# State-space stage: step sizes one state sooner; second mixer: the gates' logarithm first, query expansions behind the gate rows

## The chip, the cores and the metric

The kernel runs on one core of one Trainium2 chip. Times are device microseconds of one execution. The engines are TensorE (PE, matmuls; PEld is its weight load), VectorE (DVE), ScalarE (ACT), GpSimd (POOL) and SyncE (SP). Each works through its own list of instructions in order, and semaphores tie the lists together.

## The reference

A decoder of four layers, each with two mixers and a feed-forward part, over x of 16 x 128 tokens x 128 channels. Two of its parts are touched. The second mixer of layer 0 (the stage `l0_mlstm` of the kernel) is an attention whose weights come from gates:

```
log_fg = log_sigmoid(f_pre);  lf_cs = cumsum(log_fg)
log_d  = lf[..., 1:, None] - lf[..., None, 1:] + i_pre[..., None, :]   # causal
m      = max(log_d);  d_mat = exp(log_d - m)
s_mat  = (q k^T / sqrt(DH)) * d_mat
denom  = max(|sum(s_mat)|, exp(-m)) + eps;   out = s_mat v / denom
```

`f_pre` and `i_pre` are the forget and the input gate, each a matmul that is then capped with a tanh. The first mixer of layer 2 (the stage `l2_mamba`) is a selective state-space layer, 256 inner channels (two halves of 128) by 16 states:

```
xc = silu(conv(x_branch));  x_dbl = xc @ W_x      # dt_low, B, C
dt = sigmoid(dt_low @ W_dt + b_dt) * 0.099 + 0.001
h  = exp(dt * A) * h + (dt * xc) * B_t;   y_t = sum(h * C_t)
y  = (y + xc * D) * silu(z);   out = y @ W_out
```

## The kernel before, in words

The stages run one after the other. Between two stages all engines meet, so a stage starts when the last engine has ended the one before it. In each stage every engine has its list written out by hand, in the order of the code.

**The gates of `l0_mlstm`.** The block that ends the stage before holds `prepare` on VectorE, constants for this stage: zeros, biases, then `minus`, `a3`, `m3` and `thrice`, which are only needed once the rows are spread. Then the stage's own block starts. TensorE makes the forget gate (`gate = 1`), then the input gate (`gate = 0`) (L1878, 64 short matmuls a gate), then one score (L1888). ScalarE takes tanh of both (L2053), then Exp and Ln of the forget gate (L2057, L2059). VectorE makes the context's statistics (`c_stats`, two halves, L192 to L204), then the gate rows: the running sum `cs` (L2144), `a_row` (L2145), the running maximum `neg_m` (L2146), `floor_row` (L2147) and the sign of `neg_m` (L2148), which sets `rows_set`. GpSimd expands the queries, `q_pair`, in four instructions (L2316), with the two halves of `c_scales` (L212) ahead of the second and the third of them. TensorE fills its waits with matmuls whose result nobody reads, `keep_clock(n)` (L1903), then spreads `a_row` and `neg_m` (L1913), subtracts what ScalarE has rounded (L1920) in two parts, and turns `floor_row` (L1924); the exponents of batch 0 stand behind that in its list, and then the loop over 16 batches.

**The state-space stage.** The 16 batches go in four quarters `q` of 512 tokens, and in each quarter over 16 states `n`; `t = 16 q + n` counts the 64 steps. In a step VectorE runs one scan per half (L2707) and feeds the first half of the next step (`feed`, L2689; in every fourth step the second half as well, L2695); GpSimd feeds the second half (L2779) in the other steps and multiplies both halves by C (`read_out`, L2786); TensorE spreads B (`spread_b`, L2459) and C (`spread_c`, L2465) over the partitions and adds what GpSimd read out (`add_state`, L2480); ScalarE copies B and C from PSUM (L2612, L2617) and makes the decays (L2604). `feed(t)` on VectorE waits for ScalarE's copy of B, and on ScalarE that copy stands behind the copy of C of the step before.

Beside this, the steps of quarter `q` prepare quarter `q+1`: four taps of convolution a half (L2409, n = 4, 5, 8, 9), the tangent (L2565), `branch_x` on VectorE (L2672, L2562 on ScalarE), `x_bc` for B and C (L2427), `x_step` for the low-rank step size (L2433), its copy `take_xd` (L2592), `steps` (L2449), `tanh` (L2597), and `step_size` on VectorE (L2667), which makes `dtx`. GpSimd's feed of the first step of a quarter waits for the second half of `dtx`. The placement of each is a condition on `n`, as in TensorE's list:

```
if n == 11:
    x_bc(q + 1)
if n == 12:
    x_step(q + 1)
    take_high(q + 1, 0)
if n == 13:
    take_high(q + 1, 1)
    steps(q + 1, 0)
```

## Time and profile before

| | |
|---|---|
| median of 3 runs | 1565.3 us (1560.38 to 1567.12) |
| the profiled execution, its own time | 1562.59 us |
| its span in the trace | 1559.7 us, 28295 instructions |
| busy: PE, DVE, ACT, POOL | 1354.9, 1179.8, 879.3, 773.8 us (87, 76, 56, 50%) |
| mean granted TensorE clock | 0.944 of full speed |
| `l0_mlstm`, from its first gate matmul to the turn of `floor_row` | 157.01 to 179.41 us |
| state-space stage, from its first scan to its last | 726.5 to 968.6 us |

The profiled execution's own time is 2.9 us above its span (what lies around the first and the last instruction), and 2.7 us below the median of the three runs. A busy PE is not PE at its peak. No engine is busy throughout, so what a change is worth has to be read from the places where engines wait for each other.

### The profile page before, as it was taken

Reading aid. Unit: us, or ns where it says so; the run is one execution under the profiler, and the core shown is the slowest. Engines: PE = TensorE matmul, PEld = TensorE weight load, DVE = VectorE, ACT = ScalarE, POOL = GpSimd, SP = SyncE. Lnnn points to the kernel's source line nnn. Section 1 sums busy time; section 2 is a strip of 40 time slices with the busy share of each in tenths; the row PEclk is TensorE's granted clock in tenths of the full one; section 3 lists DMA queues with packets and bytes.
Section 4 is the critical chain, followed back from the end, with each engine's and each line's share of the span. In section 5 each row is a group of like instructions: output and inputs, shape, how many; then the busy total and the mean of one; then the engine's idle time right before and its main releaser. Section 6 shows DMA issues by size and latency. Waiting matters only on the chain. (4 is left out here: it accounts for less than half of the span.)

```text
span 1559.7 us, 28295 instructions
## 1 busy us (share of the span) xinstructions
PE 1354.9 (87%) x9646; PEld 885.0 (57%) x9646; DVE 1179.8 (76%) x2532; ACT 879.3 (56%) x2677; POOL 773.8 (50%) x740
## 2 busy tenths in 40 slices
PE   6997887899789998898988988899998678877895
PEld 3554555555567775563333432788887434436784
DVE  7997567789777785465898998777776787887654
ACT  4774342377677773225777775577766244343663
POOL 5667353222655442414988889433336222454553
PEclk9998898999999999999999999999999798878997
DMA  7000000000000000002000000000000400001353
GB/s 312 1 2 1 1 1 1 1 2 2 1 1 2 2 2 0 1 1 97 1 1 1 0 1 1 1 2 1 2 2 6 137 1 1 1 1 53 107 162 99
DMA packets 38494, 39.48 MB, mean 25 GB/s; under 512 B 2128, under 2 KB 35536, under 8 KB 37584
## 3 DMA queue, kind: packets, MB, share of 16 engines
q1 hardware_dynamic: 36304, 33.48, 6.5%
q0 software_dynamic: 2048, 4.20, 0.9%
q8 instruction: 78, 1.28, 0.3%
q14 instruction: 64, 0.52, 0.1%
HBM read 23.52 MB, written 14.16 MB: 24 GB/s over the span
## 5 line engine op out<-in xcount | busy, mean ns | idle before, releaser
L837 POOL TENSOR_TENSOR l_xattn_probs<-l_xattn_probs,l_xattn_recip 128x512 f32<-128x512 f32 x128 | 133.1, 1040 | 220.1 <-DVE l_xattn_recip L776 219.8
L1055 ACT ACTIVATE l_attn_probs<-ps,l_attn_neg_max 128x128 f32<-128x128 f32 x512 | 145.2, 383 | 64.0 <-DVE l_attn_neg_max L1126 62.7
L2786 POOL TENSOR_TENSOR l_mamba_hc<-l_mamba_h,l_mamba_c 128x512 f32<-128x512 f32 x128 | 159.0, 1270 | 0.0
L2707 DVE TENSOR_TENSOR_SCAN l_mamba_h<-ps,l_mamba_dBx 128x512 f32<-128x512 f32 x128 | 152.7, 1213 | 1.8 <-ACT ps L2604 0.7
L2480 PE MATMUL ps<-l_mamba_hc,w_const 128*128 128x512 f32 x256 | 136.3, 638 | 19.2 <-POOL l_mamba_hc L2786 16.5
L771 DVE COPY l_xattn_probsT<-ps 128x512 f32<-128x512 f32 x128 | 88.0, 687 | 69.7 <-PE ps L623 69.7
L246 POOL TENSOR_TENSOR rs<-rs,neg_half 128x4 f32<-128x4 f32 (+1 forms) x32 | 43.4, 1357 | 151.8 <-DVE rs L240 151.7
L722 ACT ACTIVATE l_xattn_probs<-ps,l_xattn_neg_max 128x128 f32<-128x128 f32 x256 | 91.8, 388 | 41.3 <-DVE l_xattn_neg_max L766 41.3
L722 ACT ACTIVATE l_xattn_probs<-l_xattn_biased,l_xattn_neg_max 128x128 f32<-128x128 f32 x256 | 99.3, 391 | 12.2 <-DVE l_xattn_neg_max L766 12.2
L2604 ACT ACTIVATE ps<-l_mamba_th,l_mamba_w_a_bias,l_mamba_w_a_scale 128x508 f32<-128x508 f32 x128 | 97.1, 782 | 13.4 <-DVE l_mamba_h L2707 12.9
L2480 PEld LDWEIGHTS ps<-l_mamba_hc,w_const 128*128 128x128 f32 x256 | 44.8, 194 | 86.7 <-POOL l_mamba_hc L2786 69.3
L623 PE MATMUL ps<-w_const,l_xattn_probs 128*128 128x128 f32 x512 | 81.7, 283 | 9.4 <-DVE l_xattn_probsT L771 5.3
L1126 DVE TENSOR_REDUCE l_attn_neg_max<-ps 128x8 f32<-128x1024 f32 x64 | 77.9, 1218 | 14.1 <-PE ps L926 13.9
L623 PEld LDWEIGHTS ps<-w_const,l_xattn_probs 128*128 128x128 f32 x512 | 57.4, 142 | 51.2 <-issue 39.3
L2779 POOL TENSOR_TENSOR l_mamba_dBx<-l_mamba_dtx,l_mamba_b 128x512 f32<-128x512 f32 x48 | 61.0, 1271 | 45.3 <-DVE l_mamba_dtx L2667 24.8
L1182 POOL TENSOR_TENSOR l_attn_probs<-l_attn_probs,l_attn_row_recip 128x1024 f32<-128x1024 f32 x32 | 60.7, 1896 | 40.6 <-DVE l_attn_row_recip L1074 40.6
L937 PEld LDWEIGHTS ps<-w_const,l_attn_probs 128*128 128x128 f32 x512 | 56.4, 142 | 42.2 <-issue 30.1
L937 PE MATMUL ps<-w_const,l_attn_probs 128*128 128x128 f32 x512 | 69.3, 279 | 7.9 <-DVE l_attn_probsT L1141 6.0
L615 PE MATMUL ps<-l_xattn_k,l_xattn_q 64*128 64x128 f32 x1024 | 74.4, 285 | 1.6 <-ACT xnT L381 0.9
L926 PE MATMUL ps<-l_attn_k_one,l_attn_q 32*128 32x512 f32 x256 | 73.1, 647 | 0.0
L615 PEld LDWEIGHTS ps<-l_xattn_k,l_xattn_q 64*128 64x128 f32 x1024 | 62.1, 187 | 11.8 <-issue 8.0
L261 POOL TENSOR_SCALAR xn<-x,mean,rs 128x128 f32<-128x128 f32 x67 | 56.2, 849 | 10.8 <-POOLq L123 8.7
(595 smaller groups left out, 3638.3 us busy)
## 6 DMA issues: line engine op xcount, KB each, us to landing
sorted_in<-l_nothing SPq DMA_DIRECT2D x4, 1344.0 KB, 11.5
sorted_out<-l_wide SPq DMA_DIRECT2D x8, 512.0 KB, 3.9
w_early<-in_l_moe SPq DMA_DIRECT2D x1, 3688.0 KB, 12.0
l_large<-sorted_in SPq DMA_DIRECT2D x4, 576.0 KB, 6.3
w_l_xattn<-in_l_xattn SPq DMA_DIRECT2D x1, 2176.0 KB, 18.7
l_large<-sorted_in SPq DMA_DIRECT2D x4, 512.0 KB, 4.4
w_early<-in_l_xattn SPq DMA_DIRECT2D x1, 1890.0 KB, 11.8
sorted_out<-l_wide SPq DMA_DIRECT2D x4, 320.0 KB, 2.6
```

The source lines that it names most:

```text
L615: mm = nc.tensor.matmul(S_of(D, n)[:, i * P:(i + 1) * P], q_sb[rows, b % 2, c, :], k_sb[rows, b % 2, c if own else 0, :], start=True, stop ...
L623: mm = nc.tensor.transpose(T_of(n)[:, g * P:(g + 1) * P], probs[:, D % 2, n, g, :], G.c["ident"])
L722: ins = nc.scalar.activation(probs[:, D % 2, n, g, :], values, ACT.Exp, bias=neg_max[:, D % 2, n, g:g + 1], accum_out=row_sum[:, D % 2, n, ...
L771: nc.vector.tensor_copy(probsT[:, D % 2, n, :, :], heads4(T_of(n))).then_inc(copied, 1)
L837: nc.gpsimd.tensor_tensor(probs[:, D % 2, n, :, :], probs[:, D % 2, n, :, :], along(recip[:, D % 2, n, :], [P, HALF, P]), ALU.mult).then_i ...
L937: mm = nc.tensor.transpose(T_all[:, g * P:(g + 1) * P], probs[:, t % 4, g, :], G.c["ident"])
L1055: ins = nc.scalar.activation(probs[:, t % 4, g, :], S_of(t)[:, g * P:(g + 1) * P], ACT.Exp, bias=neg_max[:, t % 2, g:g + 1], accum_out=total)
L1126: nc.vector.tensor_reduce(neg_max[:, t % 2, :], by_head(S_of(t), 8), AX.X, ALU.max, negate=True).then_inc(maxed, 1)
L2480: nc.tensor.matmul(G.ps[:, SUM_BANK[half], :], G.c["ident"], hc[:, t % 4, half, :], start=False, stop=n == NS - 1).then_inc((sum0, sum1)[h ...
L2604: nc.scalar.activation(bank4(DA_BANK[half])[:, :, 1:], th[:, q % 2, half, :, 1:], ACT.Exp, scale=a_scale[:, half, n:n + 1], bias=a_bias[:, ...
L2707: nc.vector.tensor_tensor_scan(flat(h[:, t % 2, half, :, :]), G.ps[:, DA_BANK[half], :], flat(dBx[:, t % 2, half, :, :]), 0.0, ALU.mult, A ...
L2786: nc.gpsimd.tensor_tensor(heads4(hc[:, t % 4, half, :]), h[:, t % 2, half, :, :], c_sb[:, t % 3, :, :], ALU.mult).then_inc((hc0_set, hc1_s ...
```

## The change

It has two parts. In `l0_mlstm`, the second half of `prepare` moves into VectorE's own list of the stage (`prepare_split`), ScalarE takes the forget gate through tanh, Exp and Ln before the tanh of the input gate, VectorE sets `rows_set` before it makes `floor_row` and makes the second half of the context's statistics after the rows, GpSimd's second, third and fourth `q_pair` wait until the rows are made, and TensorE has 6 instead of 14 `keep_clock` matmuls and starts to spread `a_row` before `neg_m` is there.

```diff
+        def prepare_split(dve):
+            link = Link(dve, prepared, 2)
             for n in range(2):
                 link.note(nc.vector.tensor_scalar(minus[:, n, :], G.c["ident"][0:R3, 0:R3], -1.0, None, ALU.mult))
             link.catch()
...
             score(0)
-            pe.wait_ge(gates_set, 2)
-            keep_clock(14)
-            pe.wait_ge(rows_set, 1)
+            pe.wait_ge(gates_set, 1)
+            keep_clock(6)
             for n, row in enumerate((a_row, neg_m)):
+                if n == 0:
+                    pe.wait_ge(own, 2)
+                else:
+                    pe.wait_ge(rows_set, 1)
...
-            for n, gate in enumerate((gate_f, gate_i)):
-                act.wait_ge(gates_made, n + 1)
-                nc.scalar.activation(gate[:], G.ps[:, G_BANK[1 - n], 0:P], ACT.Tanh, bias=bias15[:, 1 - n:2 - n],
-                                     scale=1.0 / CAP).then_inc(gates_set, 1)
+            act.wait_ge(gates_made, 1)
+            nc.scalar.activation(gate_f[:], G.ps[:, G_BANK[1], 0:P], ACT.Tanh, bias=bias15[:, 1:2], scale=1.0 / CAP).then_inc(gates_set, 1)
             act.wait_ge(gates_set, 1)
-
             nc.scalar.activation(gate_f[:], gate_f[:], ACT.Exp, scale=-CAP).then_inc(gates_set, 1)
-            act.wait_ge(gates_set, 3)
+            act.wait_ge(gates_set, 2)
             nc.scalar.activation(gate_f[:], gate_f[:], ACT.Ln, bias=1.0).then_inc(logs_set, 1)
+            act.wait_ge(gates_made, 2)
+            nc.scalar.activation(gate_i[:], G.ps[:, G_BANK[0], 0:P], ACT.Tanh, bias=bias15[:, 0:1], scale=1.0 / CAP).then_inc(gates_set, 1)
...
-            for half in range(2):
-                c_stats(dve, half)
+            prepare_split(dve)
+            c_stats(dve, 0)
             dve.wait_ge(logs_set, 1)
-            dve.wait_ge(gates_set, 2)
             link(nc.vector.tensor_tensor_scan(cs[:], G.ones[:, 0:P], gate_f[:], 0.0, ALU.mult, ALU.add))
+            dve.wait_ge(gates_set, 3)
             link(nc.vector.scalar_tensor_tensor(a_row[:], gate_i[:], CAP, cs[:], ALU.mult, ALU.add))
             link(nc.vector.tensor_tensor_scan(neg_m[:], zeros[:], a_row[:], NEG, ALU.add, ALU.max))
-            link(nc.vector.tensor_tensor(floor_row[:], cs[:], neg_m[:], ALU.subtract))
-            nc.vector.tensor_scalar(neg_m[:], neg_m[:], -1.0, None, ALU.mult).then_inc(rows_set, 2)
+            nc.vector.tensor_scalar(neg_m[:], neg_m[:], -1.0, None, ALU.mult).then_inc(rows_set, 1)
+            dve.wait_ge(rows_set, 1)
+            nc.vector.tensor_tensor(floor_row[:], cs[:], neg_m[:], ALU.add).then_inc(rows_set, 1)
+            c_stats(dve, 1)
...
-                if q in (1, 2):
-                    c_scales(pool, q - 1)
+                if q == 1:
+                    c_scales(pool, 0)
+                    pool.wait_ge(rows_set, 2)
+                if q == 3:
+                    c_scales(pool, 1)
```

In the state-space stage, `x_bc` is split in its two halves and starts one state sooner, `x_step`, `take_xd`, `steps`, `tanh` and `step_size` come one state sooner, the second tangent follows its copy in state 9 and VectorE's use of it comes between the two scans of state 10; and `spread_c` goes ahead of the second of a step's two `add_state`.

```diff
-                if n == 0 and q > 0:
-                    add_state(t - 2, 1)
-                    add_state(t - 1, 0)
                 if n == 3:
                     add_state(t - 2, 0)
-                if n >= 3:
+                if n >= 3 or (n == 0 and q > 0):
                     add_state(t - 2, 1)
-                    add_state(t - 1, 0)
                 if t < LAST:
                     spread_c(t + 1)
+                if n >= 3 or (n == 0 and q > 0):
+                    add_state(t - 1, 0)
...
+                    if n == 10:
+                        x_bc(q + 1, 1)
                     if n == 11:
-                        x_bc(q + 1)
+                        x_bc(q + 1, 0)
+                        x_step(q + 1)
                     if n == 12:
-                        x_step(q + 1)
                         take_high(q + 1, 0)
+                        steps(q + 1, 0)
                     if n == 13:
                         take_high(q + 1, 1)
-                        steps(q + 1, 0)
-                    if n == 14:
                         steps(q + 1, 1)
...
-                    if n in (7, 10):
-                        tangent_x({7: 1, 10: 0}[n])
-                    if n == 12:
+                    if n in (7, 9):
+                        tangent_x({7: 1, 9: 0}[n])
+                    if n == 11:
                         take_xd(q + 1)
-                    if n in (13, 14):
-                        tanh(q + 1, n - 13)
+                    if n in (12, 13):
+                        tanh(q + 1, n - 12)
...
-                if n == NS - 1 and q + 1 < NQ:
-                    step_size(q + 1, 1)
                 if t < LAST:
                     feed(t + 1)
+                if n == 10 and q + 1 < NQ:
+                    branch_x(q + 1, 0)
                 scan(t, 1)
-                if n == NS - 2 and q + 1 < NQ:
-                    step_size(q + 1, 0)
+                if n in (NS - 3, NS - 2) and q + 1 < NQ:
+                    step_size(q + 1, n - (NS - 3))
```

How the built instructions stand, at three places. First, ScalarE from the end of the stage before to the turn of the rows, before:

```order
L487 COPY xnT<-ps 128x512 x4
L123 UNCONDITIONAL_BRANCH
L2049 UNCONDITIONAL_BRANCH
L2053 ACTIVATE l_mlstm_gate_f<-ps,l_mlstm_bias 128x128
L2053 ACTIVATE l_mlstm_gate_i<-ps,l_mlstm_bias 128x128
L2057 ACTIVATE l_mlstm_gate_f<-l_mlstm_gate_f 128x128
L2059 ACT_TABLE_LOAD
L2059 ACTIVATE l_mlstm_gate_f<-l_mlstm_gate_f 128x128
L2066 CAST l_mlstm_high<-ps 96x512 x4
L2069 CAST l_mlstm_a<-ps 96x512
L2069 CAST l_mlstm_m<-ps 96x512
L2071 ACT_TABLE_LOAD
```

The same place in the changed kernel:

```order
L2058 ACTIVATE l_mlstm_gate_f<-ps,l_mlstm_bias 128x128
L2060 ACTIVATE l_mlstm_gate_f<-l_mlstm_gate_f 128x128
L2062 ACT_TABLE_LOAD
L2062 ACTIVATE l_mlstm_gate_f<-l_mlstm_gate_f 128x128
L2064 ACT_TABLE_LOAD
L2064 ACTIVATE l_mlstm_gate_i<-ps,l_mlstm_bias 128x128
L2071 CAST l_mlstm_high<-ps 96x512 x4
L2074 CAST l_mlstm_a<-ps 96x512
L2074 CAST l_mlstm_m<-ps 96x512
L2076 ACTIVATE l_mlstm_floor_row<-l_mlstm_floor_row 128x128
```

There are two loads of a function table in both. The first stays ahead of the Ln; the second has moved from the Exp of `floor_row` to the tanh of the input gate.

Second, GpSimd in the same stretch, before:

```order
L2316 TENSOR_TENSOR l_mlstm_q_pair<-xnT,w_const 128x1024
L209 MEMSET l_mlstm_neg_half 128x16
L212 TENSOR_TENSOR l_mlstm_rs<-l_mlstm_ve,l_mlstm_neg_half 128x8
L2316 TENSOR_TENSOR l_mlstm_q_pair<-xnT,w_const 128x1024
L212 TENSOR_TENSOR l_mlstm_rs<-l_mlstm_ve,l_mlstm_neg_half 128x8
L2316 TENSOR_TENSOR l_mlstm_q_pair<-xnT,w_const 128x1024 x2
```

The same place in the changed kernel:

```order
L2326 TENSOR_TENSOR l_mlstm_q_pair<-xnT,w_const 128x1024
L209 MEMSET l_mlstm_neg_half 128x16
L212 TENSOR_TENSOR l_mlstm_rs<-l_mlstm_ve,l_mlstm_neg_half 128x8
L2326 TENSOR_TENSOR l_mlstm_q_pair<-xnT,w_const 128x1024 x2
L212 TENSOR_TENSOR l_mlstm_rs<-l_mlstm_ve,l_mlstm_neg_half 128x8
L2326 TENSOR_TENSOR l_mlstm_q_pair<-xnT,w_const 128x1024
```

The second and third expansion now stand together behind a wait for the rows, and the second half of the scales has moved one expansion down.

Third, TensorE in states 11 to 13 of a quarter (L2480 adds a state, L2465 spreads C, L2459 spreads B, L2427 is `x_bc`, L2433 `x_step`, L2440 `take_high`, L2449 `steps`), before:

```order
L2465 MATMUL ps<-l_mamba_bc,rows_bf 128x512
L2427 MATMUL ps<-l_mamba_xc,l_mamba_w_w_bc 96x512 x2
L2459 MATMUL ps<-l_mamba_bc,rows_bf 128x512
L2480 MATMUL ps<-l_mamba_hc,w_const 128x512 x2
L2465 MATMUL ps<-l_mamba_bc,rows_bf 128x512
L2433 MATMUL ps<-l_mamba_xc,w_l_mamba 128x512 x2
L2440 MATMUL ps<-l_mamba_high,l_mamba_w_minus 96x512
L2459 MATMUL ps<-l_mamba_bc,rows_bf 128x512
```

States 10 to 12 in the changed kernel, where these lines are L2490, L2475, L2469, L2436 and L2443:

```order
L2490 MATMUL ps<-l_mamba_hc,w_const 128x512
L2436 MATMUL ps<-l_mamba_xc,l_mamba_w_w_bc 96x512
L2469 MATMUL ps<-l_mamba_bc,rows_bf 128x512
L2490 MATMUL ps<-l_mamba_hc,w_const 128x512
L2475 MATMUL ps<-l_mamba_bc,rows_bf 128x512
L2490 MATMUL ps<-l_mamba_hc,w_const 128x512
L2436 MATMUL ps<-l_mamba_xc,l_mamba_w_w_bc 96x512
L2443 MATMUL ps<-l_mamba_xc,w_l_mamba 128x512 x2
L2469 MATMUL ps<-l_mamba_bc,rows_bf 128x512
```

The spread of C now stands between the two additions of a step, and three matmuls of preparation (half of `x_bc`, both of `x_step`) stand ahead of state 12's spread of B, where there were two.

## Rows read from the trace of the kernel before

**Rows 1.** Timeline of VectorE, gate rows: start us, us, engine, line, what [idle before <-releaser]

```profile
155.31 0.31 DVE L1852 TENSOR_SCALAR l_mlstm_minus<-w_const 96x96 bf16<-96x96 f32 x2
...
165.22 0.42 DVE L2144 TENSOR_TENSOR_SCAN l_mlstm_cs<-ones,l_mlstm_gate_f 128x128 f32<-128x128 f32 x1 [0.93 <-DVE l_mlstm_mean L204]
165.68 0.29 DVE L2145 SCALAR_TENSOR_TENSOR l_mlstm_a_row<-l_mlstm_gate_i,l_mlstm_cs 128x128 f32<-128x128 f32 x1
166.01 2.14 DVE L2146 TENSOR_TENSOR_SCAN l_mlstm_neg_m<-l_mlstm_zeros,l_mlstm_a_row 128x128 f32<-128x128 f32 x1
168.18 1.80 DVE L2147 TENSOR_TENSOR l_mlstm_floor_row<-l_mlstm_cs,l_mlstm_neg_m 128x128 f32<-128x128 f32 x1
170.09 0.71 DVE L2148 TENSOR_SCALAR l_mlstm_neg_m<-l_mlstm_neg_m 128x128 f32<-128x128 f32 x1
```

**Rows 2.** Timeline of ScalarE, the gates

```profile
155.35 0.59 ACT L487 COPY xnT<-ps 128x512 f32<-128x512 f32 x1 [1.19 <-PE ps L474]
160.71 0.37 ACT L2053 ACTIVATE l_mlstm_gate_f<-ps,l_mlstm_bias 128x128 f32<-128x128 f32 x1 [4.78 <-PE ps L1878]
162.95 0.37 ACT L2053 ACTIVATE l_mlstm_gate_i<-ps,l_mlstm_bias 128x128 f32<-128x128 f32 x1 [1.87 <-PE ps L1878]
...
163.53 1.28 ACT L2059 ACT_TABLE_LOAD   x1
164.82 0.31 ACT L2059 ACTIVATE l_mlstm_gate_f<-l_mlstm_gate_f 128x128 f32<-128x128 f32 x1
...
177.76 1.28 ACT L2071 ACT_TABLE_LOAD   x1
```

**Rows 3.** Timeline of GpSimd, third and fourth query expansion

```profile
165.97 3.86 POOL L2316 TENSOR_TENSOR l_mlstm_q_pair<-xnT,w_const 128x1024 f32<-128x1024 f32 x2
```

**Rows 4.** Timeline of TensorE, from the first gate matmul to the turn

```profile
157.01 0.66 PE L1878 MATMUL ps<-xnT,l_mlstm_wq 128*32 128x128 f32 x8 [1.70 <-PEq L123]
...
163.46 3.19 PE L1903 MATMUL ps<-mask_kq_bf,ident_bf 128*128 128x512 bf16 x14
170.85 1.20 PE L1913 MATMUL ps<-l_mlstm_a_row,l_mlstm_thrice 128*96 128x128 f32 x8 [4.20 <-DVE l_mlstm_neg_m L2148]
...
179.41 0.33 PE L1924 MATMUL ps<-w_const,l_mlstm_floor_row 128*128 128x128 f32 x1 [1.43 <-ACT l_mlstm_floor_row L2071]
```

**Rows 5.** Windows: stretch, its us, busy us of PE, PEld, DVE, ACT, POOL, PEclk

```profile
171.85:174.84 2.99, 2.99 (x14) 2.14 (x12) 0.00 (x0) 1.16 (x2) 1.46 (x5) 0.50 0.00 0
```

**Rows 6.** Timeline of VectorE, quarter 1 into quarter 2 (states 10 to 2)

```profile
830.63 0.69 DVE L2672 SCALAR_TENSOR_TENSOR l_mamba_xc<-ps,l_mamba_xc 128x512 f32<-128x512 f32 x1 [0.77 <-ACT ps L2565]
...
835.38 0.66 DVE L2689 TENSOR_TENSOR l_mamba_dBx<-l_mamba_dtx,ps 128x512 f32<-128x512 f32 x1
...
839.70 0.69 DVE L2689 TENSOR_TENSOR l_mamba_dBx<-l_mamba_dtx,ps 128x512 f32<-128x512 f32 x1 [1.22 <-ACT l_mamba_b L2612]
...
845.19 1.34 DVE L2667 SCALAR_TENSOR_TENSOR l_mamba_dtx<-l_mamba_th,l_mamba_xc 128x512 f32<-128x512 f32 x1
...
847.77 0.66 DVE L2667 SCALAR_TENSOR_TENSOR l_mamba_dtx<-l_mamba_th,l_mamba_xc 128x512 f32<-128x512 f32 x1
...
856.05 0.69 DVE L2689 TENSOR_TENSOR l_mamba_dBx<-l_mamba_dtx,ps 128x512 f32<-128x512 f32 x1 [1.95 <-ACT l_mamba_b L2612]
```

**Rows 7.** Timeline of ScalarE, the same stretch

```profile
838.12 0.59 ACT L2592 COPY l_mamba_y<-ps 128x512 f32<-128x512 f32 x1 [1.13 <-PE ps L2433]
...
854.95 0.59 ACT L2617 COPY l_mamba_c<-ps 128x512 f32<-128x512 f32 x1 [2.79 <-PE ps L2465]
```

**Rows 8.** Timeline of GpSimd, the same stretch

```profile
848.51 1.27 POOL L2779 TENSOR_TENSOR l_mamba_dBx<-l_mamba_dtx,l_mamba_b 128x512 f32<-128x512 f32 x1 [2.54 <-DVE l_mamba_dtx L2667]
```

**Rows 9.** Timeline of TensorE, the same stretch

```profile
831.70 1.88 PE L2427 MATMUL ps<-l_mamba_xc,l_mamba_w_w_bc 128*96 128x512 f32 x4
...
836.20 1.88 PE L2433 MATMUL ps<-l_mamba_xc,w_l_mamba 128*128 128x512 f32 x4
...
851.06 3.63 PE L2480 MATMUL ps<-l_mamba_hc,w_const 128*128 128x512 f32 x4 [1.58 <-POOL l_mamba_hc L2786]
```

More of the change, by code:

```diff
@@ L2421, in z_branch, with x_bc @@
                                  G.xnT[:, q * QUAD:(q + 1) * QUAD, :], start=True, stop=True).then_inc(z_made, 1)
-            def x_bc(q):
-                pe.wait_ge(xc_set, 2 * (q + 1))
-                for half in range(2):
-                    mm = nc.tensor.matmul(G.ps[0:3 * M, BC_BANK, :], w_bc[:, half, :, :].rearrange("p n m -> p (n m)"),
-                                          xc[:, half, :, :], start=half == 0, stop=False, skip_group_check=True)
-                mm.then_inc(bc_raw, 1)
+            def x_bc(q, half):
+                pe.wait_ge(xc_set, 2 * q + 2 - half)
+                mm = nc.tensor.matmul(G.ps[0:3 * M, BC_BANK, :], w_bc[:, half, :, :].rearrange("p n m -> p (n m)"),
+                                      xc[:, half, :, :], start=half == 1, stop=False, skip_group_check=True)
+                if half == 0:
+                    mm.then_inc(bc_raw, 1)
             def x_step(q):
@@ L2499, in _ @@
             keep_clock(nc, G, 4, 6)
-            x_bc(0)
+            x_bc(0, 1)
+            x_bc(0, 0)
             x_step(0)
@@ L2760, in _ @@
                         branch_x(q + 1, 1)
-                    if n == 10:
-                        branch_x(q + 1, 0)
             gated(NQ - 1)
```

## The prediction

> **What bounds the kernel now.** The page comes first: no engine is busy over 87% and the stages run one behind the other, so a microsecond taken out of one stage's chain of waits is a microsecond at the end, unless the stage has a second chain just behind. I therefore read the timelines engine by engine at the two places of the change.
>
> In the second mixer the reader is to see a chain that goes around all engines. TensorE starts at 157.01, once all engines have met [rows 4]; ScalarE has nothing until the forget gate is made, at 160.71, and then the input gate's tanh at 162.95 stands ahead of the forget gate's Exp, table load and Ln, which ends at 165.13 [rows 2]. VectorE's rows follow. Two of them are far too long: the scan of `cs` takes 0.42 us, the scan of `neg_m` over the same 128x128 takes 2.14, and the subtraction 1.80 [rows 1]. The cause is beside them: GpSimd's two query expansions run from 165.97 to 169.83 [rows 3], and both slow instructions lie inside that. TensorE runs out of its 14 filling matmuls, stands 4.20 us, and starts to spread at 170.85 [rows 4]; right after that idle time the granted clock is 0.50, the 1.2 GHz level, from 171.85 to 174.84 [rows 5]. The turn of `floor_row`, behind which the loop over batches stands, comes at 179.41 [rows 4], after one more table load of 1.28 us on ScalarE [rows 2].
>
> In the state-space stage VectorE is nearly always busy, and its pauses are what the stage loses. Per quarter there are three that the change can touch: 0.77 us for the tangent, 1.22 for the copy of B in state 13 (its feed of state 14), and 1.95 for the copy of B two steps into the next quarter [rows 6]. The last comes from a chain: the second step size is made at 847.77 [rows 6], GpSimd has then stood 2.54 us for it [rows 8], its read-outs and so TensorE's additions are late and run at the low clock, four matmul records in 3.63 us where the preparation takes 1.88 [rows 9], the spread of C stands behind them, and ScalarE waits 2.79 us for C with the copy of B next in its list [rows 7].
>
> **The change, mixer part.** (a) The moved constants begin on VectorE at 155.31 [rows 1]; without them the last engine to end is ScalarE, at 155.35 + 0.59 = 155.94 [rows 2]. The stage then starts between 155.94 and 157.01; engines need a moment to meet, so I take 156.2, a gain of 0.8. (b) ScalarE: tanh of the forget gate at 160.71 - 0.8 = 159.9. From a tanh to the table load that follows its Exp the trace has 163.53 - 162.95 = 0.58; so load at 160.5, Ln at 161.8, its end at 162.1, then the second load to 163.4, and the input gate's tanh to 163.8 [rows 2]. That second load is a new item on this path, and it has gone from 177.76. (c) VectorE: `cs` is done long before; `a_row` 0.29, to 164.15. Nothing of GpSimd runs beside it now, because its expansions wait for the rows, so `neg_m` should cost the 0.42 of `cs` and the sign between nothing and 0.71, I take `a_row`'s 0.29: rows at 164.9 [rows 1]. (d) TensorE began its 14 fillers at 163.46, hence 0.8 sooner now, and six of them cost 6 x 3.19 / 14 = 1.4 [rows 4]: it is free at 164.1, and `a_row` is there at 164.15. Its clock rises perhaps no sooner than before although it starts sooner, which can cost some tenths; I take 164.5 for the start of the spread, between 164.2 and 165. (e) From the first spread to the turn took 179.41 - 170.85 = 8.56 [rows 4]. Of that 1.28 was the load [rows 2], gone, and half of the 2.99 at the low clock, 1.5, goes if TensorE no longer stands still before it [rows 5]. 5.8 remain: the turn comes at 170.3, **9.1 us sooner**. Bounds: 6 if the low clock comes anyway and the rows keep half of their old length; 10.5 if the spread starts at 164.2 and the fillers hide more.
>
> What hides the moved work: the two expansions now begin at about 165.2 and end 3.86 later, at 169.1 [rows 3], before the turn; the scores of batch 4, the first to need one, are four batches away. The second half of the context's statistics comes behind the rows and will be slowed by those expansions, but its first reader is batch 8's context. If that cover were gone it would be one 1.93 us expansion on the path. No DMA is moved.
>
> The Trainium skill's page "ScalarE: Activation LUTs", section "What ACT_TABLE_LOAD costs", gives a switch of tables as about 2.66 us, a drain of 1.38 included. The rows have the Ln start 1.29 after the load does and show no drain [rows 2]. By the page's figure the input gate would be 1.4 later (an estimate), the load removed near the turn would be worth 1.4 more, and this part would still give about 9.
>
> **The change, state-space part.** Where a quarter ends, in us from the rows of quarter 1 into 2. State 10: the tangent comes directly behind its copy and VectorE's use of it one feed later: the 0.77 is gone. States 11 and 12: here the change costs. `x_bc`'s second half ends at about 833.0 (`x_bc` began at 831.70 as one piece of 1.88, half of it now comes before this step's spread of B); `x_step` follows at once with four records of 1.88 [rows 9], so TensorE spreads B of state 13 at 834.7. ScalarE has `take_xd` ahead of that copy now, and between them `take_high`, each about 0.5: the copy of B is ready near 836.5. VectorE wants it at 835.38 - 0.77 = 834.6 [rows 6]: a new pause of 1.9, in the place of none. By the same steps the next feed is ready at 840.0, against 839.70 before with its 1.22 of pause [rows 6], so at this point the new kernel is 0.3 behind. Then the gain: VectorE makes the second step size before the last state's first scan, at 846.8, where GpSimd has just run dry. GpSimd's feed of the next quarter starts at 847.45 instead of 848.51 [rows 8], the read-outs are 1.1 sooner, and the spread of C stands behind one addition and not two. That puts the copy of B of the third feed at 853.2, or 854.8 if the additions still run at the low clock. VectorE wants it at 856.05 - 1.95 + 0.3 = 854.4 [rows 6]. It runs at 854.4 to 854.85: 1.2 to 1.65 sooner than 856.05. Three quarters follow another: 3.6 to 5, I take **4.0**. The ends: nothing at all, if the new pause grows by another 1.4; all three pauses gone, 3.94 a quarter, 11.8 in all.
>
> A second rule of the Trainium skill speaks against a part of this: "SBUF — State Buffer", section "SBUF: two separate sides", has VectorE and GpSimd share one pair of ports, held for a whole instruction by whichever starts first, where VectorE's has two inputs in SBUF. The rows agree (`neg_m` under the expansions). As a mechanism of this kernel: a step size takes 0.66 alone and 1.34 under GpSimd's read-outs, and can lose up to a whole 1.27 [rows 6, 8]. The first is slowed before and after; if the second, now sooner, meets a read-out as well, it costs 0.7 a quarter, 2 in all.
>
> **The sum.** 9.1 + 4.0 = 13.1. Against the profiled execution's own 1562.6 that is 1549.5; the median of the runs is 2.7 higher, at 1552.2. I predict the middle, 1551.
>
> **The rivals.**
> Only the mixer pays: the pause at states 11 to 13 eats the state-space gain. For it: TensorE has three preparing matmuls in one state. Against: it had room at the quarter's end. Time 1551 + 4 = 1555, and with the loss of the port wait 1557.
> Only half of the mixer's gain: the rows are sooner but the spread is not, because six fillers do not carry TensorE to 164.2 and the clock falls. For it: after 4.20 us idle the clock did fall [rows 4, 5]. Against: the fillers end at 164.1. Gain 4.5 + 4, time 1555.5.
> The step size's port wait alone: 1553, inside the likeliest case's range.
> More: all three pauses vanish, 20.9, time 1543.
> Slower: ScalarE's list blocks. `take_xd` waits for `x_step` with two copies of B behind it; if VectorE then lost 1.9 not once but in each of states 12 to 15, with nothing given back, a quarter would cost 7.6, 22.8 in all, against 9.1: 1551 + 4 + 22.8 = 1578. It decides from 3.0 us a quarter, which eats the 9.1. Against it: preparation in states 14 and 15 is now nil, so TensorE catches up.
>
> **How the numbers follow.** A measurement of this kernel tells about 0.5% (7.8 us) from no change. Likeliest case 0.62, own range 1547 to 1555; only the mixer 0.18; half of the mixer 0.10; more 0.07; slower or equal 0.03. The first and the fourth, and most of the second and third, gain over 7.8 us: faster 0.84, same 0.14, slower 0.02. The range reaches to 1558 (the second and third cases with 1 or 2 us on top) and to 1544.
>
> **What would show it.** In the trace of the changed kernel: `neg_m` at 0.4 us and no TENSOR_TENSOR of 1.8 ahead of the spread; the spread at 164 to 165 and TensorE's wait before it under 1 us; no granted 0.50 between spread and turn; the turn near 170; in the state-space stage no pause for the tangent, a pause of about 2 us at the feed of state 13, GpSimd's wait for `dtx` at 1.5 instead of 2.54, and less than half a microsecond of VectorE's pause two steps into a quarter. The prediction is wrong if the turn lies later than 173, or if the scans' first-to-last time, 242 us now, does not shrink.

## The result, and the profile after

| | before | changed |
|---|---|---|
| median | 1565.21 us (5 runs) | 1550.24 us (5 runs) |
| profiled execution, own time | 1562.59 us | 1551.07 us |
| its span | 1559.7 us | 1549.3 us |

The ratio is 0.9915, 95% interval 0.9893 to 0.9938: faster by 0.6 to 1.1%. The time lies 0.8 us from the 1551 of the prediction. How the terms stand behind that is another matter: some were nearly exact, one was off by more than a factor of two, and two stages that the prediction had left alone took the difference back.

The page of the changed kernel, its busy times, against the table ahead of the prediction:

```profile
span 1549.3 us, 28280 instructions
## 1 busy us (share of the span) xinstructions
PE 1350.3 (87%) x9638; PEld 887.1 (57%) x9638; DVE 1176.8 (76%) x2532; ACT 878.7 (57%) x2677; POOL 775.4 (50%) x740
```

TensorE has eight fewer matmuls, the fillers, and VectorE is 3.0 us less busy; ScalarE and GpSimd are as busy as before, within 2 us. A change of order shows in the waits, so the timelines are the place to look.

**The mixer.** VectorE's timeline of the gate rows, which answers to [rows 1]:

```profile
156.17 2.02 DVE L1855 TENSOR_SCALAR l_mlstm_minus<-w_const 96x96 bf16<-96x96 f32 x2 [0.39 <-PEq L123]
...
162.01 0.42 DVE L2148 TENSOR_TENSOR_SCAN l_mlstm_cs<-ones,l_mlstm_gate_f 128x128 f32<-128x128 f32 x1
163.70 0.29 DVE L2150 SCALAR_TENSOR_TENSOR l_mlstm_a_row<-l_mlstm_gate_i,l_mlstm_cs 128x128 f32<-128x128 f32 x1 [1.26 <-ACT l_mlstm_gate_i L2064]
164.02 0.42 DVE L2151 TENSOR_TENSOR_SCAN l_mlstm_neg_m<-l_mlstm_zeros,l_mlstm_a_row 128x128 f32<-128x128 f32 x1
164.48 0.23 DVE L2152 TENSOR_SCALAR l_mlstm_neg_m<-l_mlstm_neg_m 128x128 f32<-128x128 f32 x1
164.74 0.29 DVE L2154 TENSOR_TENSOR l_mlstm_floor_row<-l_mlstm_cs,l_mlstm_neg_m 128x128 f32<-128x128 f32 x1
```

ScalarE's, which answers to [rows 2]:

```profile
159.57 0.37 ACT L2058 ACTIVATE l_mlstm_gate_f<-ps,l_mlstm_bias 128x128 f32<-128x128 f32 x1 [3.71 <-PE ps L1881]
...
161.60 0.31 ACT L2062 ACTIVATE l_mlstm_gate_f<-l_mlstm_gate_f 128x128 f32<-128x128 f32 x1
161.93 1.28 ACT L2064 ACT_TABLE_LOAD   x1
163.22 0.37 ACT L2064 ACTIVATE l_mlstm_gate_i<-ps,l_mlstm_bias 128x128 f32<-128x128 f32 x1
```

And TensorE's, which answers to [rows 4]:

```profile
156.17 0.66 PE L1881 MATMUL ps<-xnT,l_mlstm_wq 128*32 128x128 f32 x8 [0.93 <-PEq L123]
...
161.83 1.47 PE L1906 MATMUL ps<-mask_kq_bf,ident_bf 128*128 128x512 bf16 x6
164.04 1.11 PE L1919 MATMUL ps<-l_mlstm_a_row,l_mlstm_thrice 128*96 128x128 f32 x8 [0.74 <-DVE l_mlstm_a_row L2150]
...
169.52 0.33 PE L1930 MATMUL ps<-w_const,l_mlstm_floor_row 128*128 128x128 f32 x1
```

`neg_m` takes 0.42 us, `floor_row` 0.29; the input gate's tanh stands behind the moved load and nothing else; TensorE waits 0.74 instead of 4.20; and from its first gate matmul to the turn it is 169.52 - 156.17 = 13.35 us, where it was 179.41 - 157.01 = 22.40. This length moves with the clock at the stage's entry: over the eight executions whose mixer is exactly the changed one it lay between 12.01 (`steps_only`, gate matmuls wholly at the full clock) and 13.64 (`end_fill`, 5.3 us of granted clock 0.50 at the entry; the changed kernel had 2.9, the kernel before 4.5). The gain is many times that.

**The stages.** Windows over each stage of the kernel before, cut at TensorE's first matmul in it: the gate mixer; the first mixer of layer 1 (`l1_attn`); the state-space stage; the mixer behind it; and the rest of the program (stretch, us, busy times, granted clock):

```profile
157.00:301.35 144.35, 115.33 (x1087) 75.26 (x1088) 97.34 (x329) 49.70 (x84) 56.39 (x54) 0.91 0.00 1
301.35:415.86 114.51, 106.11 (x1006) 61.57 (x1007) 98.56 (x153) 80.42 (x292) 43.48 (x69) 0.99 0.01 1
...
706.11:977.86 271.75, 239.91 (x628) 96.17 (x628) 227.58 (x281) 181.41 (x292) 222.26 (x180) 0.96 0.04 15
977.86:1206.85 228.99, 219.45 (x2131) 186.23 (x2131) 166.61 (x362) 155.43 (x614) 87.28 (x87) 1.00 0.01 2
1206.85:1559.70 352.85, 267.85 (x1509) 192.22 (x1509) 261.14 (x706) 162.76 (x373) 145.95 (x143) 0.86 0.22 63
```

The same of the changed kernel:

```profile
156.17:292.41 136.24, 112.68 (x1080) 73.47 (x1080) 96.40 (x336) 49.53 (x84) 56.45 (x54) 0.91 0.01 1
292.41:409.80 117.39, 107.52 (x1007) 62.23 (x1007) 98.59 (x154) 80.22 (x292) 43.55 (x69) 0.97 0.01 1
...
700.19:963.32 263.13, 232.09 (x627) 95.03 (x628) 227.19 (x281) 181.56 (x292) 223.42 (x180) 0.99 0.04 15
963.32:1196.73 233.41, 223.88 (x2130) 190.34 (x2131) 166.56 (x362) 155.45 (x614) 87.28 (x87) 0.98 0.01 2
1196.73:1549.30 352.57, 268.75 (x1509) 193.34 (x1509) 260.71 (x706) 162.66 (x373) 146.16 (x143) 0.86 0.22 63
```

This is the ledger; it adds up to the 10.4 us by which the span is shorter, since the stages left out are alike within 0.14 us. The gate mixer is 8.1 us shorter and begins 0.8 us sooner; the state-space stage is 8.6 shorter; `l1_attn`, whose code is the same, is 2.9 longer, and the mixer behind the state-space stage, also untouched, 4.4 longer. In both the granted clock is lower than it was. Windows over the two places of the changed kernel show a granted clock near 0.50, the 1.2 GHz level, and a busy TensorE:

```profile
391.00:398.00 7.00, 7.00 (x50) 4.04 (x52) 4.41 (x7) 3.89 (x16) 6.82 (x9) 0.51 0.00 0
964.50:971.50 7.00, 6.27 (x31) 5.87 (x30) 3.88 (x16) 1.35 (x3) 3.08 (x4) 0.51 0.00 0
```

**A turn of a quarter.** VectorE's pauses and step sizes, quarter 1 into 2, which answer to [rows 6]:

```profile
826.85 0.69 DVE L2699 TENSOR_TENSOR l_mamba_dBx<-l_mamba_dtx,ps 128x512 f32<-128x512 f32 x1 [1.95 <-ACT l_mamba_b L2622]
830.27 0.69 DVE L2699 TENSOR_TENSOR l_mamba_dBx<-l_mamba_dtx,ps 128x512 f32<-128x512 f32 x1 [0.16 <-ACT l_mamba_b L2622]
832.14 1.52 DVE L2677 SCALAR_TENSOR_TENSOR l_mamba_dtx<-l_mamba_th,l_mamba_xc 128x512 f32<-128x512 f32 x1
837.23 0.66 DVE L2677 SCALAR_TENSOR_TENSOR l_mamba_dtx<-l_mamba_th,l_mamba_xc 128x512 f32<-128x512 f32 x1
```

GpSimd's wait there, which answers to [rows 8]:

```profile
837.97 1.26 POOL L2787 TENSOR_TENSOR l_mamba_dBx<-l_mamba_dtx,l_mamba_b 128x512 f32<-128x512 f32 x1 [0.72 <-DVE l_mamba_dtx L2677]
```

The new pause of 1.95 at the feed of state 13 is there. The pause for the tangent and the one two steps into the next quarter are gone, and GpSimd stands 0.72 us instead of 2.54, where 1.5 was forecast. From the first scan's start to the last's it is 952.81 - 720.06 = 232.75 us instead of 242.0; 0.7 of these 9.3 us are lost again outside the scans.

### The profile page after: what moved, and what is told of

Its sections match the earlier page's. It is cut to its first block and busy times, and to the rows that moved or that the text cites. A ratio compares the mean times of both kernels' runs of the same rounds, so it can differ in the third digit from the quotient of the medians.

```text
span 1549.3 us, 28280 instructions
## 1 busy us (share of the span) xinstructions
PE 1350.3 (87%) x9638; PEld 887.1 (57%) x9638; DVE 1176.8 (76%) x2532; ACT 878.7 (57%) x2677; POOL 775.4 (50%) x740
## 3 DMA queue, kind: packets, MB, share of 16 engines
q8 instruction: 78, 1.28, 0.4%
## 5 line engine op out<-in xcount | busy, mean ns | idle before, releaser
L2490 PE MATMUL ps<-l_mamba_hc,w_const 128*128 128x512 f32 x256 | 135.6, 616 | 16.9 <-POOL l_mamba_hc L2794 16.3
L2490 PEld LDWEIGHTS ps<-l_mamba_hc,w_const 128*128 128x128 f32 x256 | 43.6, 189 | 76.8 <-POOL l_mamba_hc L2794 62.8
L615 PEld LDWEIGHTS ps<-l_xattn_k,l_xattn_q 64*128 64x128 f32 x1024 | 62.1, 187 | 11.8 <-issue 8.1
L714 ACT COPY l_xattn_oT<-ps 128x512 f32<-128x512 f32 x64 | 37.9, 593 | 42.6 <-PE ps L636 36.4
## 6 DMA issues: line engine op xcount, KB each, us to landing
sorted_in<-l_nothing SPq DMA_DIRECT2D x4, 1344.0 KB, 11.5
w_early<-in_l_moe SPq DMA_DIRECT2D x1, 3688.0 KB, 11.8
```

Source lines behind the costliest of these rows:

```text
L615: mm = nc.tensor.matmul(S_of(D, n)[:, i * P:(i + 1) * P], q_sb[rows, b % 2, c, :], k_sb[rows, b % 2, c if own else 0, :], start=True, stop ...
L2490: nc.tensor.matmul(G.ps[:, SUM_BANK[half], :], G.c["ident"], hc[:, t % 4, half, :], start=False, stop=n == NS - 1).then_inc((sum0, sum1)[h ...
```

## The experiments

There were twelve runs, two of them repeats of the kernel before and of the changed one. Of each, one execution was profiled. Those of experiments 3 to 8 were timed in that execution alone, so their verdicts rest on lengths inside the trace and not on the time.

**1 to 3. One part at a time, and the kernel before once more.** `mixer_only` has the first diff alone, `ssm_only` the second alone, `before_again` neither.

> The change's first part alone; the state-space stage is that of the kernel before. Theory (the two parts add): the turn of floor_row at 169.5 us as in the changed kernel, the stage l0_mlstm about 8 us shorter than its 144.3, the state-space stage at its 271 to 272 us of before; time about 8 to 9 us under the kernel before, ratio 0.9945. Rival (the saving is given back behind, in the next stage, where the changed kernel's profile is 2.9 us longer than before): ratio 0.997 or more, and the stage l1_attn again near 117.4 us.

> The change's second part alone; the mixer is that of the kernel before. Theory of the prediction as it was sized: state-space stage 4 us shorter than 271.8. Theory after the changed kernel's profile: 8.6 us shorter, about 263, because the granted clock no longer falls at each turn of a quarter; then ratio about 0.9945. Rival (part of the 8.6 is the phase in which this one execution met the clock, not the order of work): 266 to 268 us.

> The kernel before, unchanged, profiled a second time. It tells how much a stage whose code nobody touched moves from one execution to the next. If the 2.9 us more in l1_attn and the 4.4 us more in the stage behind the state-space stage come from stretches of low clock that fall differently each time, then these two stages differ from 114.5 and 229.0 us by some us here too, each by as much as its stretches at 0.50; if they come from the change, both stages are again within 0.5 us of these lengths.

They ran on a chip where the kernel before takes 1596.09 us. Its gate mixer (144.31 us) and `l1_attn` (114.52) are within 0.04 us of the first profile. The stage behind the state-space stage is not: 230.62 instead of 228.99, with 3.4 us of granted clock 0.50 in it where the first profile has none. So of the two outcomes that were expected, `l1_attn` gives the second and this stage a mild form of the first. What is much longer is the last part of the program, 386.34 instead of 352.85, which has most of the DMA traffic:

```profile
159.88:304.19 144.31, 115.30 (x1088) 75.22 (x1088) 97.35 (x329) 49.69 (x84) 56.48 (x54) 0.91 0.00 1
304.19:418.71 114.52, 106.12 (x1006) 61.58 (x1007) 98.54 (x153) 80.42 (x292) 43.56 (x69) 0.99 0.01 1
708.93:981.04 272.11, 240.53 (x627) 96.29 (x628) 227.52 (x281) 181.39 (x292) 222.31 (x180) 0.96 0.04 15
981.04:1211.66 230.62, 221.08 (x2131) 187.85 (x2131) 166.55 (x362) 155.43 (x614) 87.41 (x87) 0.99 0.01 2
1211.66:1598.00 386.34, 282.07 (x1509) 203.91 (x1509) 260.72 (x706) 162.82 (x373) 145.88 (x143) 0.83 0.20 57
```

`mixer_only` had the ratio 0.9956 (0.9936 to 0.9976), `ssm_only` 0.9958 (0.9940 to 0.9975). Their gains, 0.44 and 0.42%, each known to 0.2%, add to the 0.85% of the whole. In `mixer_only` the stage is 136.37 us, 7.9 shorter, as the theory had it, and the state-space stage has its 271.87. But the ratio lies between the theory's 0.9945 and the rival's 0.997 and its interval holds both, and `l1_attn` took 117.48, as the rival had it. So 3 of the 8 us were given back in this execution, and not all of them. `ssm_only` has the 263 of the second theory; its rival's 266 to 268 is refuted. By stage, `l1_attn`, state space and the mixer behind it:

```profile
303.51:420.95 117.44, 107.55 (x1006) 62.29 (x1007) 98.62 (x153) 80.22 (x292) 43.64 (x69) 0.97 0.01 1
711.17:974.40 263.23, 232.09 (x628) 95.02 (x628) 227.22 (x281) 181.53 (x292) 223.58 (x180) 0.99 0.04 15
974.40:1207.81 233.41, 223.89 (x2130) 190.34 (x2131) 166.60 (x362) 155.43 (x614) 87.44 (x87) 0.98 0.01 2
```

So 263.2 and 233.4 both belong to the second diff. But `l1_attn` has its longer length, 117.44, here too, where the mixer ahead of it is the old one. The 2.9 us can come without the mixer's edit.

**4. Expansions beside the rows again.**

```diff
                     c_scales(pool, 0)
-                    pool.wait_ge(rows_set, 2)
```

> The changed kernel, but GpSimd's second and third query expansion don't wait for the rows. From the first gate matmul to the turn of floor_row the kernel before took 22.40 us and the changed one 13.35. Theory (the expansions held VectorE's instructions with two inputs in SBUF): a_row or neg_m again takes about 2 us, the spread starts 2 to 4 us later and the turn is at 15.5 to 17 us. Rival (the rows were slow because ScalarE's and TensorE's order was another, and the expansions are innocent): rows at 0.29, 0.42, 0.23 and the turn at 13.4.

VectorE's timeline of this kernel:

```profile
164.43 1.63 DVE L2150 SCALAR_TENSOR_TENSOR l_mlstm_a_row<-l_mlstm_gate_i,l_mlstm_cs 128x128 f32<-128x128 f32 x1 [1.26 <-ACT l_mlstm_gate_i L2064]
166.09 2.00 DVE L2151 TENSOR_TENSOR_SCAN l_mlstm_neg_m<-l_mlstm_zeros,l_mlstm_a_row 128x128 f32<-128x128 f32 x1
```

The long rows are back with nothing changed but what GpSimd runs beside them. That shows the cause of the long rows. The turn is at 174.67 - 156.61 = 18.06 us, more than forecast: TensorE now stands twice, 1.16 and 1.18 us, the granted clock is 0.50 over 169 to 172, and 0.3 us are the entry, at the low clock as long as in `end_fill` (13.64). Of the 4.7 us at the turn 2.9 are left at the stage's end (139.13 against 136.24).

**5. Both tanh first again** (ScalarE's list as in the kernel before).

> The changed kernel, but ScalarE takes both tanh first, as before; the second table load is back ahead of the Exp of floor_row. Theory: a_row about 0.7 us later, and the 1.28 us load back on the chain, the turn at 15.3 us after the first gate matmul instead of 13.35. Rival (a load is hidden in either place, the gain is the clock's and the expansions'): 13.4 to 14.

The turn came 175.63 - 159.36 = 16.27 us after the first gate matmul, 2.9 later than in the changed kernel. Half of it lies behind `a_row`, 7.23 instead of 5.82 us to the turn, with the load of 1.28 ahead of `floor_row`. The other half lies before it: `cs` starts 8.58 us into the stage instead of 5.84, since Exp, load and Ln stand behind the input gate, and `a_row` starts 1.5 later. The theory holds, its size was low; 0.3 of it are the gate matmuls, which were at the low clock longer in this execution, as long as in `end_fill` (13.64).

**6. No fillers.** `keep_clock(6)` ahead of the spread becomes `keep_clock(0)`.

> The changed kernel with no filling matmuls between the first score and the spread of a_row: TensorE then stands about 2.2 us there instead of 0.74. Theory of the prediction (an idle TensorE brings the low clock into the spread): granted clock 0.50 somewhere between spread and turn, the turn up to 1.5 us later than 13.35, at 14.5 to 15. Rival (2.2 us idle are not enough for that, 6 fillers aren't needed): 13.35, clock 1.00.

TensorE stood 2.28 us and started the spread at the full clock; from the start of `a_row` (163.76) to the turn (169.64) it is 5.88 us, against 5.82 in the changed kernel. Its turn came 12.07 us after the first gate matmul, sooner than the 13.35 for another reason: this execution entered the stage at the full clock. `steps_only`, which has the six fillers and entered in the same way, took 12.01. My theory is refuted and the rival holds: at this length of wait the fillers buy nothing. Two waits of 1.2 in experiment 4 were followed by a low clock, one of 2.28 here was not, so the length of a wait alone does not foretell it.

**7 and 8. The two edits of the state-space stage apart.** `swap_only` has just `spread_c` ahead of the second addition, `steps_only` everything else of the second diff; both have the new mixer.

> The mixer of the changed kernel, and of the state-space part only the place of spread_c, ahead of the second addition. The state-space stage took 271.8 us before and 263.1 in the changed kernel. Theory (the swap gives the small gains in the ordinary steps, the earlier step sizes give the turns of the quarters): 2 to 3.5 us of the 8.6, the stage at 268.5 to 270, GpSimd's wait for dtx at each turn still 2.5 us. Rival (the swap gives most of it, since the wait for C at the turn was behind the additions): 265 or less.

> The changed kernel with spread_c put back behind both additions: the earlier preparation and step sizes alone. The state-space stage took 271.8 us without either, 266.4 with the swap alone, 263.15 with both. Theory (the two edits add): 268.5 us. Rival (an earlier step size pays only if C is also spread sooner, since the pause at the turn is C's; or the other way round, either alone removes the same pause): 270 or more in the first case, 266 or less in the second. And whether the stage behind it is 229.0 or 233.4 tells if the low clock there goes with the swap alone.

| state-space stage | us | of it at granted clock 0.50 | mixer behind it |
|---|---|---|---|
| neither (`mixer_only`) | 271.87 | 20.4 | 228.98 |
| `swap_only` | 266.40 | 20.5 | 233.42 |
| `steps_only` | 266.90 | 10.3 | 233.43 |
| both (changed kernel) | 263.13 | 6.8 | 233.41 |

The swap gives 5.5 alone, the earlier steps 5.0, both 8.7, 1.7 less than the sum; why they overlap is not shown. The swap gave more than its theory had, and so did the steps, 5.0 for 3.3; neither stage length is one that a theory or a rival had named. The swap takes away none of the low clock, the earlier steps half of it, so part of what they give is the clock's.

GpSimd's wait for `dtx` is still 2.34 to 2.54 us at the three turns of `swap_only`, as the theory had it, and the swap does not pay at the turn as such. At the second turn ScalarE waits 1.44 us for C, where the kernel before has 2.79, but then 1.55 for B, and VectorE's pause is 2.24, longer than the 1.94 of `mixer_only`. The third turn has the same instructions at the full clock, and a pause of 0.18. These are windows over the two turns, with granted clock 0.50 and 1.00, and rows inside them:

```profile
844.00:849.00 5.00, 4.80 (x7) 1.96 (x8) 3.25 (x4) 1.68 (x4) 5.00 (x5) 0.50 0.00 0
846.74 0.59 ACT L2625 COPY l_mamba_c<-ps 128x512 f32<-128x512 f32 x1 [1.44 <-PE ps L2475]
848.87 0.59 ACT L2620 COPY l_mamba_b<-ps 128x512 f32<-128x512 f32 x1 [1.55 <-PE ps L2469]
849.49 0.69 DVE L2697 TENSOR_TENSOR l_mamba_dBx<-l_mamba_dtx,ps 128x512 f32<-128x512 f32 x1 [2.24 <-ACT l_mamba_b L2620]
...
904.00:909.00 5.00, 2.99 (x8) 0.89 (x7) 4.82 (x5) 3.34 (x6) 5.00 (x5) 1.00 0.00 0
909.01 0.69 DVE L2697 TENSOR_TENSOR l_mamba_dBx<-l_mamba_dtx,ps 128x512 f32<-128x512 f32 x1 [0.18 <-ACT l_mamba_b L2620]
```

Counted by the start of each step's first scan, `swap_only` gains 6.0 us on `mixer_only` (the whole stage only 5.5, since 1.2 more lie behind its last scan): 4.6 in ordinary steps, some tenths at a time, 2.1 at the third turn, and it loses 0.4 and 0.3 at the other two. And the low clock in the next stage comes with either.

**9 to 12. The changed kernel again, and two tries to win back what it left.** `end_fill` adds fillers at the end of the stage:

```diff
+                if q == NQ - 1 and n >= 9:
+                    keep_clock(nc, G, 7, 3)
...
+            keep_clock(nc, G, 7, 6)
             project_out(NQ - 1, 0)
             project_out(NQ - 1, 1)
+            keep_clock(nc, G, 7, 6)
```

`respaced` spreads the preparation (`x_step` now takes the halves that it is to do):

```diff
                     if n == 11:
                         x_bc(q + 1, 0)
-                        x_step(q + 1)
+                        x_step(q + 1, (1,))
                     if n == 12:
+                        x_step(q + 1, (0,))
                         take_high(q + 1, 0)
-                        steps(q + 1, 0)
                     if n == 13:
                         take_high(q + 1, 1)
-                        steps(q + 1, 1)
+                        steps(q + 1, 0)
+                    if n == 14:
+                        steps(q + 1, 1)
...
+                if t < LAST:
+                    copy_b(t + 1)
                 if q + 1 < NQ:
                     if n in (12, 13):
                         take_high(q + 1, n - 12)
                     if n == 14:
                         take_bc(q + 1)
-                if t < LAST:
-                    copy_b(t + 1)
...
-                    if n == 11:
+                    if n == 12:
                         take_xd(q + 1)
-                    if n in (12, 13):
-                        tanh(q + 1, n - 12)
+                    if n in (13, 14):
+                        tanh(q + 1, n - 13)
```

> The changed kernel, unchanged, on another day or chip. Theory (each stage's length belongs to the kernel): 136.2 for l0_mlstm, 263.1 for the state-space stage, 233.4 for the stage behind it, each within 0.3 us; l1_attn is the one that may be 114.4 or 117.4. Rival (the 4.4 us more behind the state-space stage are chance): 229.0 there this time.

> The changed kernel plus filling matmuls that nobody reads on TensorE: 3 in each step from state 9 of the last quarter, 6 before and 6 after the last project_out. Theory (the stage behind the state-space stage is 4.4 us longer because TensorE is too little busy at the end of it, after the swap, and enters at the low clock): clock 1.00 there, that stage at 229.0, the state-space stage within 1 us of 263.1; time about 4 us below the changed kernel. Rival (the low clock comes anyway, or the fillers delay the additions): 233.4 and a state-space stage of 264 or more.

> The changed kernel with the preparation spread out: one x_step matmul each in states 11 and 12, steps in states 13 and 14, and on ScalarE the copy of B ahead of take_high, take_xd in state 12. Theory (the pause of 1.95 us at the feed of state 13 comes from three preparing matmuls and two copies ahead of B's): that pause under 0.5 us, 0.5 to 1.2 us a quarter shorter, state-space stage at 260 to 261.5. Rival (TensorE's whole work in states 8 to 13 is the limit; the pause only moves to state 14): 263 or more, with a pause above 1 us at state 14.

> Both edits together: if each does what its theory says, about 6 us below the changed kernel; by the rivals no better than it.

| | median | ratio to before (95%) | state space | behind it | rest |
|---|---|---|---|---|---|
| before, same chip | 1563.65 | 1 | | | |
| `after_again` | 1552.86 | 0.9925 (0.9900 to 0.9950) | 263.18 | 233.40 | 351.93 |
| `end_fill` | 1548.47 | 0.9899 (0.9871 to 0.9926) | 263.40 | 230.55 | 355.97 |
| `respaced` | 1551.86 | 0.9904 (0.9873 to 0.9935) | 261.92 | 230.60 | 356.26 |
| `respaced_fill` | 1546.16 | 0.9885 (0.9856 to 0.9915) | 262.17 | 230.61 | 353.95 |

`after_again` repeats each of these stages within 0.1 us, and the last part within 0.7: the 4.4 us behind the state-space stage are no chance of one execution. `end_fill` keeps the full clock at the entry and wins 2.85 of them for 0.2 in its own stage, so its theory holds by two thirds: the rest is a second low stretch near the end of that stage, which stays. That rest is no mark of the change: the kernel before has it too in `before_again` (230.62). `respaced` gets 1.3 us out of its own stage, 261.9, just outside its theory's 260 to 261.5. The pause of 1.95 at the feed of state 13 is down to 0.35, with 0.52 at a scan behind it, but a new one of 1.07 has come at the first step size, which now waits for its tanh:

```profile
833.04 1.21 DVE L2680 SCALAR_TENSOR_TENSOR l_mamba_dtx<-l_mamba_th,l_mamba_xc 128x512 f32<-128x512 f32 x1 [1.07 <-ACT l_mamba_th L2610]
```

It too has 230.6 behind it, with no filler at all. So fillers are one way to that entry and not the only one; which activity decides it these runs don't say. And the last part of the program is 2 to 4 us longer in all three, again with a lower clock in it (0.85 instead of 0.86), so their spans gain less than these two stages do. By time `respaced_fill` has the best ratio, 0.9885, and its median is 6.7 us below `after_again`, where 6 was expected; but its profiled execution is only 3.2 below, and the intervals of all four overlap. None is shown to be faster than the changed kernel.

## Why the prediction was right, point by point

**Start of the stage, 0.8 sooner.** `before_again` and `mixer_only` give it by themselves: from the transposes (L474) to the first gate matmul 6.02 and 5.25 us, 0.77. Right in the mechanism. In the changed kernel's own profile the 0.84 are 1.22 at this place, with the transposes at the full clock, less 0.38 lost earlier in the program.

**ScalarE's order and the table load.** Predicted 163.4 for the start of the input gate's tanh, measured 163.22; experiment 5 shows the order's worth. The page "ScalarE: Activation LUTs" of the Trainium skill (section "What ACT_TABLE_LOAD costs") would have had a drain on top. The trace does not agree: in the changed kernel each load takes 1.28 us, its function starts 1.29 to 1.30 after the load does, and the instruction ahead ended 0.02 or less before it.

**The rows.** Predicted 164.9, measured 164.71; the cause, GpSimd's expansions, is shown by experiment 4. The rule of the Trainium skill's page "SBUF — State Buffer", section "SBUF: two separate sides", agrees with it as far as instructions with two inputs in SBUF go: `a_row` took 1.63 beside an expansion and 0.29 clear of it, `neg_m` 2.00 and 0.42.

**The spread and the turn.** Predicted 164.5 and 170.3, measured 164.04 and 169.52. Some 0.3 us of that is luck: the entry was at the low clock for 2.9 us and not for 4.5, and the forget gate's tanh came 3.40 us after the first gate matmul and not 3.70. What I gave as the danger, a low clock for want of fillers, was no danger (experiment 6). At the stage's end 8.1 of the 9.05 us within the stage are left. The other 0.95 goes with the clock in the loop over batches, and not with the edit: from the turn to the stage's end it is 121.8 to 121.9 us in the four executions with 17 us of low clock in the loop (the kernel before twice, `both_tanh_first`, `end_fill`) and 122.8 to 122.95 in the nine with 20.5, of which `ssm_only` has the old mixer. `expansions_beside` alone stands outside, 121.1 with 17.

**The state-space stage, 4.0: mis-sized, it measured 8.6, outside the 3.6 to 5 of my working.** The steps that I worked out are there: the tangent's pause is gone, the new pause is 1.95 (predicted 1.9), the second step size ran alone at 0.66, and GpSimd is served sooner. The third feed of a quarter runs 11.26 us sooner than before in quarter 2 and 8.95 sooner in quarter 1, a gain of 2.3 a quarter and not 1.3. Two things are missing in my sum. I priced the swap of `spread_c` only at the turn, and it pays in the ordinary steps, 4.6 us over the stage, 0.7 of them in the last quarter, which has no turn (experiment 7). And I had the read-outs 1.1 us sooner at the turn where GpSimd's wait shrank by 1.8. Of the low clock at the turns the earlier steps alone leave one stretch of three, both edits none, the swap alone two; how much of the 8.6 is the order and how much the clock no run separates.

**The term that was not in the sum.** "A microsecond taken out of one stage's chain of waits is a microsecond at the end" was the sentence that failed. Stages behind, with the same code, had more low clock: +4.4 behind the state-space stage, to 233.4 in all eight executions with a changed order in that stage and neither respacing nor fillers at its end (the old order had 229.0 twice and 230.6 once, so against its longer length it is +2.8), and +2.9 in `l1_attn`, which is a coin with two sides (below). 4.0 predicted against 8.6 - 4.4 = 4.2 found is agreement by two errors that cancel.

The closeness of the total is in part luck as well. For the median the change was worth 15.0 us, for the two profiled executions 11.5; the sum was 13.1. I had put the profiled execution at 1549.5 and the median 2.7 above it; the one was 1551.07, and the median lay 0.8 below it. The 1551 that I gave stands between two forecasts that missed by 1.6 and 2.0 us on opposite sides.

**The rivals.** The port wait of the second step size did not come: it took 0.66 to 0.77 us. The pause at states 11 to 13 did not eat the gain, and the mixer did not stop at half. ScalarE's list did block once a quarter, for 1.95 to 2.14, then for 0.36 or less, and not again. The case with more, all three pauses gone, was priced at 11.8 us in this stage; the 8.6 lie nearer to it than to the 4.0, though one pause stayed.

## What to carry to other kernels

Look beside an instruction that takes several times what its twin takes: what another engine ran in the same microseconds was worth more here than any shortening of the chain itself. In a loop where each engine has its own list, an instruction that waits for the slowest partner should stand behind all that others wait for (the spread of C behind one addition, not two, was one moved line and 5.5 us in that stage, of which the next one took 4.4 back). And compare a change stage by stage, untouched stages too: the sum of the touched ones is not the result when the clock ahead of the next stage depends on how this one ends.

## What the runs showed of the hardware that I had not expected

Ahead of the last part, stages with the same code repeat within 0.4 us from chip to chip, but some have two or three lengths, each with its own amount of low clock. `l1_attn` took 114.3 to 114.6 us in six executions and 117.3 to 117.5 in eight, the longer ones each with some 7 us of granted clock 0.50 near its end, the shorter ones each with 3.4 us at its start (one longer one, `mixer_only`, has both); both lengths occur with the old mixer ahead (114.51 and 117.44), and what chooses is open. The stage behind the state-space stage took 229.0 us with no low clock in it, 230.6 with 3.4 us and 233.4 with 10.2.

A VectorE instruction with one input was slow beside an expansion as well: `minus` (96x96, f32 to bf16) takes 0.31 us for two before and 2.02 in the changed kernel, where it has moved next to `q_pair`. It costs nothing there, and no run moves it alone, so that the expansion holds it is argued and not shown. Not every instruction is slowed: the statistics of the context (one input, 128x128, L192) take 1.64 us for eight beside two expansions and 1.61 clear of them. So each kind has to be read from its own rows.

The chip of experiments 1 to 3 gave 386.3 us to the last part of the program where the first gave 352.9, and 2.9 us more to the part ahead of the mixer; of the stages between, all but one were alike to 0.4 us. A comparison between chips would have hidden this change twice over. On that chip the last part, with the same code, was also 7.0 us shorter in the profile of `mixer_only` (379.3), so two single profiles from there say nothing of a gain of this size.
